# Attention scores shifted by VectorE in every second step, and the gates mixed tile by tile

## The chip, the cores and the metric

The kernel runs on one core of one Trainium2 chip. The metric is the device time of one execution in microseconds. Three runs of the kernel before gave 3368.48, 3369.95 and 3369.95 us; the median is 3369.95 us.

## The reference, cut to what matters

Two layers of graph network and feed-forward block over 3327 nodes with 256 features. The change touches only the last feed-forward block's attention. It has 4 heads (64 wide each) with 4 experts per head: for each head the keys and values are shared, the queries differ by expert, and a causal softmax is taken over 3327 positions. A gate (softmax over the 4 experts) mixes the experts' outputs.

```python
q = einsum('bnsd,neod->bneso', sx, wq); k = einsum('bnsd,nod->bnso', sx, wk); v = einsum('bnsd,nod->bnso', sx, wv)
att = softmax(einsum('bnesd,bntd->bnest', q, k) * d ** 0.5 + causal, axis=-1)
qkv = where(pad[:, :, None], 0.0, einsum('bnest,bntd->bnesd', att, v))
out = transpose(qkv, (0, 1, 3, 2, 4)).reshape(b, nh, s, ne * d)
gs = softmax(einsum('bnsf,nef->bnse', out, gate_w) + gate_b[None, :, None, :], axis=-1)
mixed = einsum('bnsed,bnse->bnsd', out.reshape(b, nh, s, ne, d), gs)
```

The inputs are float32 and so is the softmax. A row's maximum must be known before its exponentials are taken.

## The kernel before, in words

**Units.** `stage_attention` works on two heads at a time (a pair `hp`, 0 or 1). The 3328 positions are cut into query blocks `b`: block 0 has 256 columns, blocks 1 to 6 have 512. A unit `(hp, b, e)` is one query block of one expert `e` for both heads (in block 0 two experts share a unit). There are 52 units. Unit (hp, b, e) has 4b + 2 groups, one for each tile `t` of 128 keys that the block may see, two groups to a step: 1, 3, 5, 7, 9, 11 and 13 steps in blocks 0 to 6. That makes 776 groups. "Units of five steps or more" are those of blocks 2 to 6: 40 units. In a unit the last three groups are narrower (384, 256 and 128 of the 512 columns) because of the causal mask.

**One group.** TensorE makes the scores of 128 keys by 512 queries for both heads (`scores`, L1749: three passes of high and low halves, `klo*qhi`, `khi*qlo`, `khi*qhi`; L1752: a fourth pass that multiplies ones by `nm`, the row of negated maxima, and so subtracts each query's maximum; L1758 adds the causal mask in the diagonal groups). Each pass is two matmuls, one for each head, that run side by side. ScalarE takes the exponential from PSUM into `pt` (L1843, four buffers). TensorE multiplies by the values (`values`, L1770) and GpSimd adds `pt` into the denominators `acc` (`add_up`, L2052; the first group of a unit is a copy, L2049). In the last two units VectorE does that sum instead (L1956).

**Row maxima.** Two units ahead, TensorE makes scores with queries as rows (`row_max`, L1736), and VectorE takes their maxima (L1906, L1910, L1915, L1917). These pieces and the scores share three PSUM slots in a fixed rotation (`slot_users`, `take_slot`): each user waits until the reader of three users ago is done.

**Order of a step** (loops written out by hand, one for each engine): TensorE does [a turn of the next unit's maxima], the first piece of row maxima, the scores of groups g+2 and g+3, the remaining pieces (one or two), the late turns, then the values of groups g and g+1. Turns are small jobs through `psX`: new keys ("k"), new queries ("q"), the row of maxima ("r") and the unit's result ("t"). VectorE does the pieces, then its part of the turns, then a piece of the gates. Each engine's queue is in order.

**Gates.** Once the four experts of a block are done, `gate_pieces` places three pieces on the first unit of the next block, in steps 2, 3 and 4 where it has five steps or more. Piece 0 on VectorE (L1966 to L1979) makes the logits, ScalarE takes their exponential, piece 1 (L1983 to L1986) makes the weights `wgt`, GpSimd multiplies the whole block by them (L2059, 128x2048), and piece 2 on VectorE sums the four experts (L1991), adds them to `hn` (L1997), and takes the statistics for the layer norm (L2001, L2005), all for the whole block.

## Time and profile before

| What | Value |
|---|---|
| Median of three runs | 3369.95 us |
| Profiled execution's own time | 3364.28 us |
| Its span, first to last instruction | 3362.6 us |
| Instructions | 45520 |
| TensorE busy | 2953.1 us (88%) |
| VectorE busy | 1898.3 us (56%) |
| ScalarE busy | 1254.0 us (37%) |
| GpSimd busy | 1772.2 us (53%) |
| TensorE's mean granted clock | 0.934 |

The attention stage runs from about 1095 us (first exponential at 1095.5) to about 3215 us. Busy time is the union of an engine's instructions. Idle time in square brackets or behind a bar is that of the engine just before the instruction, with the instruction whose end released it.

### The profile page before, as it was taken

How to read it: one execution, taken by the hardware profiler on the slowest of the kernel's cores; microseconds unless marked ns; L12 is line 12 of the kernel's file. 1: busy time of each engine (PE TensorE's matmuls, PEld its weight loads, DVE VectorE, ACT ScalarE, POOL GpSimd, SP SyncE). 2: the span in 40 equal slices, each digit the busy share in tenths (PEclk: the TensorE clock that was granted, in tenths of full speed). 3: DMA queues.
4: the chain of work that ended last, by engine and by line, in shares of the span. 5: the costliest groups of instructions: out<-in, count | busy, mean ns of one | idle time of the engine just before them, and what ended most of it. 6: DMA issues, size and time to landing. Idle time of an engine off the chain costs nothing. (4 is left out here: it accounts for less than half of the span.)

```text
span 3362.6 us, 45520 instructions
## 1 busy us (share of the span) xinstructions
PE 2953.1 (88%) x17338; PEld 1822.7 (54%) x17338; DVE 1898.3 (56%) x3632; ACT 1254.0 (37%) x1712; POOL 1772.2 (53%) x956
## 2 busy tenths in 40 slices
PE   7998987679997889899999999788988999999953
PEld 3467666468885455555555555455555554545532
DVE  3555764487733465665655651245656565565566
ACT  2232320355633233343434344323433443434433
POOL 0030020233220357778889899636687888888014
PEclk9999888889998899999999999888999999999976
DMA  9961100299970000000000000000000000000001
GB/s 391 423 246 41 63 1 8 87 290 282 268 130 18 1 1 1 1 1 1 1 1 1 1 4 1 1 1 1 1 1 1 1 1 1 1 1 1 1 8 36
DMA packets 63624, 195.20 MB, mean 58 GB/s; under 512 B 8244, under 2 KB 25010, under 8 KB 53427
## 3 DMA queue, kind: packets, MB, share of 16 engines
q1 hardware_dynamic: 38658, 147.98, 11.4%
q0 software_dynamic: 24752, 44.31, 7.3%
q8 instruction: 143, 2.34, 0.3%
q14 instruction: 71, 0.57, 0.1%
HBM read 188.86 MB, written 3.41 MB: 57 GB/s over the span
## 5 line engine op out<-in xcount | busy, mean ns | idle before, releaser
L2052 POOL TENSOR_TENSOR at_acc<-at_acc,at_pt 128x1024 f32<-128x1024 f32 (+3 forms) x674 | 1445.8, 2145 | 257.4 <-ACT at_pt L1843 178.0
L1843 ACT ACTIVATE at_pt<-at_psR 128x1024 f32<-128x1024 f32 (+3 forms) x776 | 697.8, 942 | 993.2 <-PE at_psR L1752 686.7
L1906 DVE TENSOR_REDUCE at_mx<-at_psR 128x2 f32<-128x1024 f32 x576 | 702.1, 1225 | 493.5 <-PE at_psR L1736 492.0
L1770 PE MATMUL at_psO<-at_pt,v 128*64 128x512 f32 (+3 forms) x3104 | 716.5, 584 | 2.1 <-DVE at_oT L1939 1.8
L1736 PE MATMUL at_psR<-at_khi,at_qhi 64*128 64x512 f32 (+3 forms) x1568 | 353.5, 447 | 134.4 <-DVE at_mx L1906 91.4
L1736 PEld LDWEIGHTS at_psR<-at_khi,at_qhi 64*128 64x128 f32 x1568 | 155.8, 189 | 411.8 <-issue 360.2
L1770 PEld LDWEIGHTS at_psO<-at_pt,v 128*64 128x64 f32 x3104 | 194.2, 140 | 339.6 <-issue 239.1
L1316 PE MATMUL ga_acc<-h,ga_ring 128*128 128x257 f32 (+1 forms) x1352 | 304.7, 385 | 31.0 <-ACT ga_ring L1210 27.3
L1749 PE MATMUL at_psR<-at_qhi,at_klo 64*128 64x512 f32 (+2 forms) x1552 | 307.8, 392 | 6.6 <-ACT at_pt L1843 5.7
L1316 PEld LDWEIGHTS ga_acc<-h,ga_ring 128*128 128x128 f32 (+1 forms) x1352 | 257.3, 192 | 76.6 <-ACT ga_ring L1210 36.0
L1749 PE MATMUL at_psR<-at_qlo,at_khi 64*128 64x512 f32 (+2 forms) x1552 | 294.7, 375 | 0.0
L1749 PE MATMUL at_psR<-at_qhi,at_khi 64*128 64x512 f32 (+2 forms) x1552 | 294.0, 374 | 0.0
L1752 PE MATMUL at_psR<-at_nm,at_ones_r 64*128 64x512 f32 (+2 forms) x1552 | 293.3, 372 | 0.0
L1189 POOL DMA_DIRECT2D ga_ring<-in_adjT x91 | 110.2, 1381 | 252.5 <-DVE ga_ring L1252 247.3
L1910 DVE TENSOR_REDUCE at_mx<-at_psR 128x2 f32<-128x256 f32 (+1 forms) x152 | 102.9, 677 | 185.0 <-PE at_psR L1736 185.0
L345 PE MATMUL gc_acc<-gc_cols,gc_xs 128*128 128x512 f32 x416 | 182.8, 602 | 22.8 <-DVE gc_xs L413 12.6
L1749 PEld LDWEIGHTS at_psR<-at_qhi,at_klo 64*128 64x128 f32 x1552 | 149.2, 188 | 54.0 <-issue 39.2
L1749 PEld LDWEIGHTS at_psR<-at_qhi,at_khi 64*128 64x128 f32 x1552 | 148.6, 187 | 27.2
L1752 PEld LDWEIGHTS at_psR<-at_nm,at_ones_r 64*128 64x128 f32 x1552 | 148.4, 186 | 27.0
L1210 ACT ACTIVATE ga_ring<-ga_ring,f 128x512 f32<-128x512 f32 (+1 forms) x182 | 114.6, 682 | 128.7 <-DMA ga_ring<-in_adjT 128.7
L1749 PEld LDWEIGHTS at_psR<-at_qlo,at_khi 64*128 64x128 f32 x1552 | 148.8, 187 | 24.8
L345 PEld LDWEIGHTS gc_acc<-gc_cols,gc_xs 128*128 128x128 f32 x416 | 80.1, 193 | 124.6 <-issue 112.8
(335 smaller groups left out, 3531.3 us busy)
## 6 DMA issues: line engine op xcount, KB each, us to landing
gc_rows<-in_adj SPq DMA_DIRECT2D x26, 1664.0 KB, 17.4
ga_rows<-in_adj SPq DMA_DIRECT2D x26, 1664.0 KB, 9.9
ga_ring<-in_adjT POOLq DMA_DIRECT2D x78, 512.0 KB, 23.6
gc_cols<-in_adjT SPq DMA_DIRECT2D x26, 1024.0 KB, 14.9
gc_ring<-in_adjT SPq DMA_DIRECT2D x26, 512.0 KB, 8.2
gc_ring<-in_adjT SPq DMA_DIRECT2D x13, 256.0 KB, 2.8
ga_ring<-in_adjT POOLq DMA_DIRECT2D x13, 256.0 KB, 11.0
out_x<-X SPq DMA_DIRECT2D x6, 512.0 KB
```

Of the source, the lines that this page charges most:

```text
L345: ins = pe.matmul(acc[:, b, c, :], xs[:, t, c * P:(c + 1) * P], cols[:, t % COLS, b * BLK:(b + 1) * BLK], start=(t == 0), stop=(t == NT - 1))
L1189: pool.dma_start(ring[:, k, :, 0:w], srcT[:, k, :, c0:c0 + w], accum_op=ALU.add).then_inc(pair_added[k], 16)
L1210: ins = act.activation(ring[:, k, j, 0:w], ring[:, k, j, 0:w], ACT.Exp, bias=f20[:, 2 * k + j:2 * k + j + 1])
L1316: ins = pe.matmul(acc[:, bank(b, s), 0:DM + 1], ring[0:r, k, j, s * P:(s + 1) * P], h1[0:r, 2 * k + j, :], start=(k + j == 0), stop=last)
L1736: ins = pe.matmul(psR[:, slot, l, 0:w], qhi[lanes[l], u % 3, s * P:(s + 1) * P], khi[lanes[l], kc:kc + w], start=True, stop=True)
L1749: pe.matmul(packed(psR[:, slot, l, 0:w], g), left[lanes[l], kc:kc + P], columns(right[lanes[l], u % 3, :], g), start=first, stop=False)
L1752: ins = pe.matmul(packed(psR[:, slot, l, 0:w], g), ones_r[lanes[l], :], columns(nm[lanes[l], u % 2, :], g), start=False, stop=not diag)
L1770: ins = pe.matmul(columns(psO[lanes[l], :], g), v1[:, t, (2 * hp + l) * D:(2 * hp + l + 1) * D], packed(pt[:, g % PTS, l, 0:w], g), start= ...
L1843: act.activation(pt[:, g % PTS, :, 0:w], psR[:, slot_of["score", g] % SLOTS, :, 0:w], ACT.Exp).then_inc(e_ready, 1)
L1906: dve.tensor_reduce(mx[:, u % 2, :, s, c:c + 1].rearrange("p l o -> p (l o)"), got[:, :, 0:w], AX.X, ALU.max).then_inc(p1_read, 1)
L1910: dve.tensor_reduce(mx[:, u % 2, :, s, c:c + 1].rearrange("p l o -> p (l o)"), got[:, :, 0:w - P], AX.X, ALU.max)
L2052: pool.tensor_tensor(to, to, got, ALU.add).then_inc(added, 1)
```

## The change

In units of five steps or more, every second group but the first of these (`t` odd, `t` over 1: 320 of the 776 groups) loses the fourth pass. VectorE instead adds the negated maxima to the scores, from PSUM into `pt` (`take_shifted`), and ScalarE takes the exponential in place in `pt`. For this, each such unit has the row of negated maxima spread to all partitions once: one more pass of ones into a PSUM slot (`spread`) and a ScalarE copy into `shift`.

The gates' last part goes by tiles of 128 positions: GpSimd weighs a tile (`weigh`, steps 3 and 4), VectorE sums a tile's experts ahead of `take_shifted` in steps 5, 6, 7 and 8 counted from the block's first unit (4, 5, 5, 6 in block 2), and its statistics come at the end of that step. The add of the gate's bias disappears: the bias is a fifth column of the sum. Buffers are shared to make room.

```diff
@@ placing
+def block_weighed(u, k):
+        if ls >= 5:
+            return [(hp, b, s) for s in range(SUB) if k == 3 + s // 2]
+        return [(hp, b, s) for s in range(SUB)] if ls == 1 else []
+SUM_STEPS = {5: (4, 5, 5, 6), 7: (5, 6, 7, 8)}
+def block_summed(u, k):
+    if not u or ls < 5 or e > 1:
+        return block_weighed(u, k)
+    hp, b, _ = UNITS[u - 1 - e]
+    return [(hp, b, s) for s in range(SUB) if SUM_STEPS.get(ls, (5, 6, 7, 8))[s] == k + e * ls]
+def shifted_by_vector(g):
+    u, t, _, _ = GROUPS[g]
+    return spread_row(u) and t % 2 == 1 and t > 1
@@ slot_users
+            if k == steps_of(u) - 1 and u + 1 in SPREAD:
+                out.append(("spread", u + 1))
@@ take_slot
+                elif before in SHIFTED_UPTO:
+                    pe.wait_ge(taken, SHIFTED_UPTO[before] + 1)
@@ tensor, scores
-                    for l in range(2):
-                        ins = pe.matmul(... ones_r[lanes[l], :], columns(nm[lanes[l], u % 2, :], g), ...)
+                    if not by_vector:
+                        for l in range(2):
+                            ins = pe.matmul(... ones_r[lanes[l], :], columns(nm[lanes[l], u % 2, :], g), ...)
+                def spread(u):
+                    pe.wait_ge(x_read, turn_of["r", u] + 1)
+                    slot = take_slot(pe, ("spread", u))
+                    for l in range(2):
+                        ins = pe.matmul(psR[:, slot, l, :], ones_r[lanes[l], :], nm[lanes[l], u % 2, :], ...)
+                    ins.then_inc(b_full, 1)
@@ scalar
+                def spread(u):
+                    i = SPREAD.index(u)
+                    act.wait_ge(b_full, i + 1)
+                    if i:
+                        act.wait_ge(taken, sum(1 for g in SHIFTED if g < FIRST[u]))
+                    act.activation(shift[:, :, :], psR[:, slot, :, :], ACT.Copy).then_inc(b_ready, 1)
                 def exps(g):
+                    if g in SHIFTED_UPTO:
+                        act.wait_ge(taken, SHIFTED_UPTO[g] + 1)
+                        act.activation(pt[:, g % PTS, :, 0:w], pt[:, g % PTS, :, 0:w], ACT.Exp).then_inc(e_ready, 1)
+                        return
@@ vector
+                def take_shifted(g):
+                    dve.wait_ge(s_full, g + 1)
+                    dve.wait_ge(b_ready, SPREAD.index(u) + 1)
+                    dve.wait_ge(pv_done, g - PTS + 1)
+                    dve.wait_ge(added, g - PTS + 1)
+                    dve.tensor_tensor(pt[:, g % PTS, :, 0:w], psR[:, slot, :, 0:w],
+                                      shift[:, :, off:off + w], ALU.add).then_inc(taken, 1)
                         link(dve.tensor_reduce(gl ... gp ...))
-                        link(dve.tensor_tensor(gl[:, 0:ws, :], gl[:, 0:ws, :], gb_sb ..., ALU.add))
+                def sum_of_experts(hp, b, s):
+                    dve.wait_ge(weighed, n)
+                    dve.wait_ge(p1_read, pieces[0])
+                    link(dve.tensor_reduce(scrap, on[:, s, :, :].rearrange("p e c -> p c e"), AX.X, ALU.add))
+                    dve.tensor_tensor(there, there, scrap, ALU.add).then_inc(mix_done, 1)
@@ vector, a step
-                        for half in range(2):
-                            for piece in max_pieces(u, k, half):
-                                row_max(u + 2, *piece)
+                        for piece in max_pieces(u, k, 0):
+                            row_max(u + 2, *piece)
+                        if steps_of(u) >= 5:
+                            for x in summed:
+                                sum_of_experts(*x)
+                        if FIRST[u] + 2 * k + 3 in SHIFTED_UPTO:
+                            take_shifted(FIRST[u] + 2 * k + 3)
+                        for piece in max_pieces(u, k, 1):
+                            row_max(u + 2, *piece)
                         for x in late_turns(u, k):
                             turn(*x)
                         for x in gate_pieces(u, k):
                             gate(*x)
+                        for hp, b, s in summed:
+                            link(statistics(hp, QBLOCKS[b][0] // P + s))
@@ gpsimd
-                        pool.tensor_tensor(both, both, wgt ..., ALU.mult)      # 128x2048, a whole block
+                def weigh(hp, b, s):
+                    pool.tensor_tensor(both, both, wgt ..., ALU.mult)          # 128x512, one tile
```

## Rows read from the trace of the kernel before

**Rows 1.** The page, part 1.

```profile
PE 2953.1 (88%) x17338; PEld 1822.7 (54%) x17338; DVE 1898.3 (56%) x3632; ACT 1254.0 (37%) x1712; POOL 1772.2 (53%) x956
```

**Rows 2.** Windows of units: us, busy PE, PEld, DVE, ACT, POOL with counts, PEclk, DMA.

```profile
2615.10:2659.70 44.60, 43.20 (x302) 24.26 (x300) 23.48 (x41) 18.97 (x25) 36.86 (x17) 1.00 0.01 1
2749.90:2812.00 62.10, 54.23 (x358) 29.59 (x356) 39.64 (x73) 22.51 (x29) 50.61 (x23) 0.95 0.00 1
2812.00:2865.00 53.00, 51.60 (x358) 28.89 (x356) 28.21 (x45) 22.72 (x30) 46.08 (x22) 1.00 0.00 1
2972.60:3043.20 70.60, 62.67 (x414) 33.79 (x412) 44.75 (x77) 26.40 (x34) 60.64 (x28) 0.95 0.00 1
3043.20:3103.80 60.60, 59.75 (x414) 33.21 (x412) 32.69 (x48) 26.25 (x33) 55.29 (x26) 1.00 0.00 1
3103.80:3156.80 53.00, 52.89 (x360) 28.17 (x358) 31.82 (x37) 25.76 (x31) 3.71 (x3) 1.00 0.01 1
3156.80:3206.30 49.50, 49.50 (x338) 26.23 (x336) 29.49 (x26) 24.96 (x30) 0.00 (x0) 1.00 0.00 1
3011.50:3014.00 2.50, 2.48 (x6) 0.84 (x8) 1.46 (x5) 0.00 (x0) 2.36 (x2) 0.50 0.00 0
```

**Rows 3.** Groups by line and form on GpSimd in the attention stage.

```profile
L2052 POOL TENSOR_TENSOR at_acc<-at_acc,at_pt 128x1024 f32<-128x1024 f32 x532 | 1264.5, 2377 | 226.8 <-ACT at_pt L1843 166.4 <-POOL at_acc L2052 1.7
```

**Rows 4.** TensorE in order of time, three steps of unit (1, 6, 0).

```profile
2998.94 0.50 PE L1736 MATMUL at_psR<-at_khi,at_qhi 64*128 64x512 f32 x2
2999.74 0.39 PE L1749 MATMUL at_psR<-at_qhi,at_khi 64*128 64x512 f32 x2
2999.97 0.40 PE L1752 MATMUL at_psR<-at_nm,at_ones_r 64*128 64x512 f32 x2
3001.43 1.94 PE L1770 MATMUL at_psO<-at_pt,v 128*64 128x512 f32 x8
3003.30 0.50 PE L1736 MATMUL at_psR<-at_khi,at_qhi 64*128 64x512 f32 x2
3011.52 0.79 PE L1736 MATMUL at_psR<-at_khi,at_qhi 64*128 64x512 f32 x2 [5.86 <-DVE at_mx L1906]
3012.25 3.63 PE L1770 MATMUL at_psO<-at_pt,v 128*64 128x512 f32 x8
3015.81 0.50 PE L1736 MATMUL at_psR<-at_khi,at_qhi 64*128 64x512 f32 x2
```

**Rows 5.** VectorE in order of time, the same unit.

```profile
2993.03 1.89 DVE L1975 TENSOR_TENSOR at_gl<-at_gl,at_gb 128x32 f32<-128x32 f32 x1
3002.93 3.82 DVE L1991 TENSOR_REDUCE at_mixed<-at_on 128x512 f32<-128x2048 f32 x1 [0.16 <-POOL at_on L2059]
3006.78 1.51 DVE L1997 TENSOR_TENSOR hn<-hn,at_mixed 128x512 f32<-128x512 f32 x1
3008.33 1.11 DVE L2001 BATCH_NORM_STATS2 at_hn_stats<-hn 128x6 f32<-128x64 f32 x8
3009.47 0.64 DVE L2005 BATCH_NORM_AGGREGATE hn_mv<-at_hn_stats 128x2 f32<-128x6 f32 x8
```

**Rows 6.** GpSimd in order of time, the same unit.

```profile
2989.99 4.88 POOL L2052 TENSOR_TENSOR at_acc<-at_acc,at_pt 128x1024 f32<-128x1024 f32 x2 [0.91 <-ACT at_pt L1843]
2999.27 3.63 POOL L2059 TENSOR_TENSOR at_on<-at_on,at_wgt 128x2048 f32<-128x2048 f32 x1 [4.40 <-DVE at_wgt L1986]
```

**Rows 7.** Groups by line and form on VectorE in the attention stage.

```profile
L1906 DVE TENSOR_REDUCE at_mx<-at_psR 128x2 f32<-128x1024 f32 x576 | 702.1, 1225 | 493.5 <-PE at_psR L1736 492.0
L1887 DVE TENSOR_TENSOR at_klo<-at_psX,at_khi 128x512 fp32r<-128x512 f32 x11 | 7.6, 692 | 36.5 <-ACT at_khi L1814 36.5
L1968 DVE TENSOR_TENSOR at_gp<-at_onx,at_rden 128x128 f32<-128x128 f32 x12 | 3.5, 292 | 0.4
```

**Rows 8.** ScalarE in order of time at the end of unit (1, 4, 2).

```profile
2704.51 1.95 ACT L1843 ACTIVATE at_pt<-at_psR 128x1024 f32<-128x1024 f32 x2 [3.36 <-PE at_psR L1752]
2707.16 0.60 ACT L1818 ACTIVATE at_qhi<-at_psX 128x512 fp32r<-128x512 f32 x1 [0.70 <-PE at_psX L1701]
```

More of the change, by code:

```diff
@@ L1555, in turn_numbers, with spread_row @@
     return {x: i for i, x in enumerate(every + LAST_TURNS)}
+def shifted_by_vector(g):
+    u, t, _, _ = GROUPS[g]
+    return spread_row(u) and t % 2 == 1 and t > 1
+def spread_row(u):
+    return steps_of(u) >= 5
+SHIFTED = [g for g in range(FIRST[NU]) if shifted_by_vector(g)]
+SHIFTED_UPTO = {g: i for i, g in enumerate(SHIFTED)}
+SPREAD = [u for u in range(NU) if spread_row(u)]
 def slot_users():
@@ L1641, in block_number, with tiles_upto @@
             return hp * NQB + b
+        def tiles_upto(hp, b):
+            return sum(w // P for i in range(hp + 1) for _, w in QBLOCKS[:b if i == hp else NQB])
         def columns(ap, g):
@@ L1672, in take_slot @@
                 what, before = users[i - SLOTS]
-                pe.wait_ge(p1_read if what == "max" else e_ready, before + 1)
+                if what == "max":
+                    pe.wait_ge(p1_read, before + 1)
+                elif what == "spread":
+                    pe.wait_ge(b_ready, SPREAD.index(before) + 1)
+                elif before in SHIFTED_UPTO:
+                    pe.wait_ge(taken, SHIFTED_UPTO[before] + 1)
+                else:
+                    pe.wait_ge(e_ready, before + 1)
             return i % SLOTS
@@ L1746, in scores @@
                     diag = t * P >= QBLOCKS[b][0]
-                    for left, right, first in ((klo, qhi, True), (khi, qlo, False), (khi, qhi, False)):
+                    by_vector = g in SHIFTED_UPTO
+                    for left, right, n in ((klo, qhi, 0), (khi, qlo, 1), (khi, qhi, 2)):
                         for l in range(2):
-                            pe.matmul(packed(psR[:, slot, l, 0:w], g), left[lanes[l], kc:kc + P],
-                                      columns(right[lanes[l], u % 3, :], g), start=first, stop=False)
-                    for l in range(2):
-                        ins = pe.matmul(packed(psR[:, slot, l, 0:w], g), ones_r[lanes[l], :],
-                                        columns(nm[lanes[l], u % 2, :], g), start=False, stop=not diag)
+                            ins = pe.matmul(packed(psR[:, slot, l, 0:w], g), left[lanes[l], kc:kc + P],
+                                            columns(right[lanes[l], u % 3, :], g), start=n == 0,
+                                            stop=n == 2 and by_vector and not diag)
+                    if not by_vector:
+                        for l in range(2):
+                            ins = pe.matmul(packed(psR[:, slot, l, 0:w], g), ones_r[lanes[l], :],
+                                            columns(nm[lanes[l], u % 2, :], g), start=False, stop=not diag)
                     if diag:
@@ L1799, in _ @@
                             row_max(u + 2, *piece)
+                        if k == steps_of(u) - 1 and u + 1 in SPREAD:
+                            spread(u + 1)
                         for x in late_turns(u, k):
@@ L1863, in _ @@
                             exps(g + 3)
+                        if k == steps_of(u) - 1 and u + 1 in SPREAD:
+                            spread(u + 1)
                         for x in late_turns(u, k):
@@ new lines, in gate, with statistics @@
+                        dve.tensor_tensor(wgt[:, 0:ws, :, :], gl[:, 0:ws, :].rearrange("p s (l g) -> p s g l", l=2),
+                                          rden[:, 0:ws, 0:NE, :], ALU.mult).then_inc(gate_ready, 1)
+                def statistics(hp, tile):
+                    for l in range(2):
+                        ins = dve.bn_stats(hn_stats[:, l, :], hn[:, tile, hp * P + l * D:hp * P + (l + 1) * D])
+                    link(ins)
+                    for l in range(2):
+                        ins = dve.bn_aggr(hn_mv[:, tile, 2 * hp + l, :], hn_stats[:, l, :])
+                    return ins
@@ new lines, in last_sum @@
+                def last_sum():
+                    hp, b = NPR - 1, NQB - 1
+                    t0, n = QBLOCKS[b][0] // P, tiles_upto(NPR, 0)
+                    dve.wait_ge(weighed, n)
+                    link(dve.tensor_tensor(on[:, :, 0:2, :], on[:, :, 0:2, :], on[:, :, 2:4, :], ALU.add))
+                    link(dve.tensor_tensor(on[:, :, 0, :], on[:, :, 0, :], on[:, :, 1, :], ALU.add))
+                    there = hn[:, t0:t0 + SUB, hp * P:(hp + 1) * P]
+                    dve.tensor_tensor(there, there, on[:, :, 0, :], ALU.add).then_inc(mix_done, SUB)
+                    dve.wait_ge(mix_done, n)
+                    for s in range(SUB):
+                        link(statistics(hp, t0 + s))
@@ L2082, in _ @@
                             add_up(FIRST[u] + 2 * k + 1)
-                        for x in gate_pieces(u, k):
-                            gate(*x)
+                        for x in block_weighed(u, k):
+                            weigh(*x)
 class FfnWeights:
```

110 lines of the change are left out of this document (58 added, 52 removed).

## The prediction

> **What bounds the kernel now.** I read the page's busy times first. TensorE is busy 2953.1 us of 3362.6 and no other engine passes 56% [rows 1]. The change touches only the attention stage, so next I cut that stage into units with the windows view, since a unit's length depends on its block. Three kinds of unit stand out [rows 2].
> (a) Ordinary units. (1, 4, 1) takes 44.6 us with TensorE busy 43.20, and (1, 5, 1) takes 53.0 with 51.60, both at clock 1.00. TensorE sets their length.
> (b) Block 6. (1, 6, 1) takes 60.6 us, TensorE is busy 59.75 and GpSimd 55.29. Two GpSimd adds back to back take 4.88 us [rows 6] at a mean of 2.377 each [rows 3], so there is about 0.13 us between them. With 26 such gaps GpSimd needs 58.7 us. Its backlog from the unit before takes most of the rest, so GpSimd sets the pace of this unit. The same holds for the other block-6 units in which GpSimd adds up, six in both pairs.
> (c) First units of a block, where the previous block's gates fall. (1, 5, 0) takes 62.1 against 53.0 of its neighbour, (1, 6, 0) 70.6 against 60.6, with TensorE idle about 8 us in each.
>
> In order of time (c) becomes plain [rows 4, 5]. A plain step, from one first row-maximum piece to the next, is 2998.94 to 3003.30, 4.36 us. The step after it runs from 3003.30 to 3015.81, 12.51 us: VectorE sits 7.2 us in the last gate piece (3.82 + 1.51 + 1.11 + 0.64 and gaps), the PSUM slot isn't freed and TensorE idles 5.86 us. Then the clock stands at 0.50 of full, that is at 1.2 GHz [rows 2], and the values that took 1.94 us take 3.63. One block's last gate piece so costs 12.51 - 4.36 = 8.15 us.
>
> **The passes that go.** Two passes start at 2999.74 and 2999.97 [rows 4]: passes are pipelined, so a full one costs its pitch of 0.23 us and not its duration of 0.40. A unit of n steps loses n - 1 passes, the last two of them of 384 and 128 columns, together one full pass: n - 2 full ones. Over 8 units each of 5, 7, 9, 11 and 13 steps that is 8 x (3 + 5 + 7 + 9 + 11) = 280 passes, 64.4 us. The spread adds one pass to each of 40 units, some 0.25 us with its weights: -10. The ScalarE copy of 128x1024 takes about 1 us (two exponentials take 1.95 [rows 8]). ScalarE ends its exponentials at 2706.46 and idles 0.70 us before the copy of the new queries at 2707.16. The spread's copy fills that and moves it by some 0.35, 0.25 of which is the pass already counted: -4 in 40 units. Left: 50.4 us.
>
> **What of it doesn't reach the end.** In the six GpSimd-bound units, 11 full passes at 0.23 less the spread, about 2.3 us each, go: -13.7. Block 5's ordinary units have GpSimd at 46.08 + 22 x 0.13 = 48.9 of 53.0. In plain steps its pitch of two adds, 5.0 us, is longer than TensorE's 4.36, and four `pt` buffers cover only so much. I give back 0.5 in six units: -3. In unit (1, 6, 3) VectorE does the denominators. It will have two adds and one shifted add a step, 3 x 1.225 = 3.7 us against 49.5 / 13 = 3.8 us now, so that unit gains 1 and not 2.3: -1.3. In steps that VectorE bounds (next part), 26 outside block 6 have a pass to lose: -6. Units with three pieces in a step: -2. So 24.4 us are worth something.
>
> **The shifted add.** It is a tensor_tensor of 128x1024 with one input in PSUM and one in SBUF. The nearest rows are the same form at 512 elements, 692 ns, and a 1024-element read of PSUM, 1225 ns [rows 7]. I take 1.225; the bounds are that and that plus a whole GpSimd add (2.38), if the two engines got in each other's way. In a plain step VectorE has two pieces, 2.45 us; with the shifted add 3.7, below TensorE's 4.13. It is hidden there. The add sits between the first and the second piece in VectorE's queue, so behind it wait the later pieces, the queries' low half and the gates. The second piece's slot is next wanted one step on, by the second score group, 3.4 us after the shifted group's end, and VectorE frees it after 2.6. ScalarE's exponential then comes 1.3 us later and reads SBUF; it is busy 22.72 of 53.0, and the values that need it are a step away. Bounds for that exponential: as now, or up to 0.3 us more; neither shows.
>
> **The gates.** Removed: 8.15 us of stall and slow clock in each block. Block 6 is apart, so eight blocks: +65. Added, for a tile on VectorE: the sum 3.82 / 4 = 0.96; the add into `hn`, two SBUF inputs of 128 elements, 0.29 by [rows 7] plus a wait for GpSimd; statistics (1.11 + 0.64) / 4 = 0.44; links 0.1. That wait is the unknown. The bias add of 32 elements took 1.89 us at 2993.03 and ended at 2994.92, just after GpSimd's add at 2994.87 [rows 5, 6], a wait of 1.7. The add into `hn` of 512 elements took 1.51, against 0.69 for that size: 0.82. It can be between 0 and 2.38. I take 0.82, the row of the same instruction. A tile is then 2.6 us, and its step is 2.45 + 1.225 + 2.6 = 6.3 us for VectorE against 4.36 now: VectorE bounds it, +1.95. Four such steps cost 7.8 in block 5. In the smaller blocks some fall on a last step without a shifted add or on a step that a turn already lengthens; I take 7, 6 and 6 for blocks 4, 3 and 2. Both pairs: -54. TensorE then idles under 2.2 us at a time. At 5.86 us the clock fell afterwards, and I count on no fall here. Gate pieces 0 and 1 come behind one shifted add each, some 0.5 a block: -4. The bias add is gone, but the subtraction that ends piece 0 also has two SBUF inputs and is then the one that meets GpSimd's add: gain nothing. Sum of the gates: +7.
>
> The Trainium skill, SBUF — State Buffer, section "SBUF: two separate sides", says that VectorE and GpSimd take their shared port pair by an exclusive lock for a whole instruction, and that among 1x VectorE instructions only those with two SBUF inputs take it. The row at 2993.03 agrees (1.89 us, ending with the GpSimd add), and by that rule the shifted add (PSUM and SBUF) is free of it, as the 692 ns row has it, while four adds into `hn` in place of one take it four times.
>
> **Block 6's first units.** GpSimd waits 4.40 us for the weights and weighs in 3.63 [rows 6], and from there its adds set the time. The weights come about 1 us later and four tile multiplies have three more gaps: -3 in both pairs. Single-step and three-step units, the joint with the second pair and the tail: 0, within 3 us either way.
>
> **Sum.** 24.4 + 7 - 3 = 28 us. The profiled execution took 3364.28 us, so 3336; the median of the runs is 5.7 above it: 3342 us.
>
> **Rivals.**
> 1. The tile steps cost more than the lump did. Mechanism: each add into `hn` meets a GpSimd add early, and waits 1.7 us as at 2993.03. That is 0.88 more in 40 steps, 35 us: 3377. A whole add each time gives 1.56 x 40 = 62: 3404. It turns slower than before from 0.7 us more a tile on, a wait of 1.5. For it: the kernel repeats the same phases, and most bias adds waited so long. Against: the `hn` rows waited half that. Chance 0.20.
> 2. The tiles fit in VectorE's gaps. It idles 1.9 us in a plain step now. If the wait is nil in most and TensorE runs ahead in the slots, a tile step costs 1.1 and not 1.95: 26 us better, 3316. Chance 0.15.
> 3. GpSimd's pace spreads. With plain steps at 4.13 us and GpSimd at 5.0, blocks 4 and 5 run out of `pt` buffers, 12 units lose their pass gain of 1.5 each, and the slots cost 5 more: 3365. Chance 0.12.
> 4. The shifted adds wait for GpSimd, against the 692 ns row: 1.2 us more on average, VectorE 4.9 in a plain step, 0.5 to 0.8 over today's in some 200 steps: over 3450. Chance 0.03.
> The forecast has 0.50. That the passes aren't gone is excluded by the code.
>
> **Numbers.** A change under 0.2%, 6.7 us, can't be told from none; that is 3363 to 3377. Faster: 0.48 + 0.15 + 0.04 = 0.67. Same: 0.02 + 0.08 + 0.02 = 0.12. Slower: 0.18 + 0.03 = 0.21. The range for 8 in 10 reaches from rival 2's 3316, a little below, to past rival 1's first price: 3312 to 3386. The forecast's own is 3330 to 3358.
>
> **What would show it.** L1752's matmuls fall by 640 and 80 appear for the spread. Steps without gates in blocks 2 to 5 last 4.13 us; the (b, 1) units of blocks 4 and 5 get shorter by about 1.5 us; block 6's don't. The 5.86 us idle of TensorE is gone, with the clock at 1.00 there. In its place stand four steps of about 6.3 us in which TensorE waits for VectorE. Shifted adds are 1.22 us each. I am wrong if a plain step isn't shorter, if the `hn` adds wait over 1.5 us, if the clock falls in the tile steps, or if first units of a block stay as long as they are in every block.

## The result, and the profile after

Six runs of the kernel after gave 3383.4 to 3418.3 us, median 3391.9. Beside them six runs of the kernel before gave 3363.1 to 3370.0, median 3368.4. The ratio of the means is 1.0087, with a 95% interval of 1.0046 to 1.0128. By the medians the change made the kernel 23 us slower (29 us by the means), where 28 us faster was forecast. The profiled execution took 3411.98 us with a span of 3410.3. On a second chip the same kernel took 3408.0 against 3363.7. The kernel after scatters over 35 us and the one before over 7. In its six runs the granted clock goes with the time, from 0.928 (3418 us) to 0.940 (3383 us).

The page of the kernel after, part 1:

```profile
PE 2966.7 (87%) x16778; PEld 1797.0 (53%) x16778; DVE 2271.8 (67%) x4008; ACT 1323.7 (39%) x1754; POOL 1775.5 (52%) x992
```

Against [rows 1], TensorE has 560 matmuls less (640 gone, 80 new) and yet is busy no less. Part of that is time at the lower clock, below. VectorE has 373 us more.

Windows of the kernel after, with the columns of [rows 2]: units (1, 4, 1), (1, 5, 0), (1, 5, 1), (1, 6, 0), (1, 6, 1), (1, 6, 2) and (1, 6, 3).

```profile
2646.90:2694.00 47.10, 44.28 (x288) 23.61 (x286) 33.78 (x55) 20.61 (x27) 37.13 (x19) 0.96 0.00 1
2785.00:2852.00 67.00, 55.87 (x340) 28.99 (x340) 55.48 (x88) 24.54 (x30) 52.04 (x27) 0.95 0.00 1
2852.00:2906.40 54.40, 52.27 (x340) 27.96 (x338) 38.04 (x54) 24.60 (x30) 44.12 (x20) 0.97 0.00 1
3014.80:3088.50 73.70, 62.06 (x394) 32.10 (x393) 62.78 (x94) 28.73 (x35) 62.41 (x32) 1.00 0.00 1
3088.50:3149.30 60.80, 59.29 (x395) 32.09 (x392) 44.91 (x60) 28.37 (x33) 54.18 (x24) 1.00 0.00 1
3149.30:3200.90 51.60, 50.48 (x336) 26.11 (x334) 42.29 (x46) 28.00 (x32) 3.83 (x3) 1.00 0.00 1
3200.90:3250.10 49.20, 48.83 (x326) 24.81 (x322) 42.14 (x39) 27.40 (x31) 0.00 (x0) 1.00 0.00 1
```

First units of a block got longer, (1, 5, 0) from 62.1 to 67.0 and (1, 6, 0) from 70.6 to 73.7. VectorE is busy 55.48 and 62.78 there, where it was busy 39.64 and 44.75. The second units, which were to get shorter by 1.5, got longer too: (1, 4, 1) from 44.6 to 47.1 and (1, 5, 1) from 53.0 to 54.4. Of the units shown, the expected gain of TensorE shows only in (1, 6, 2).

**Tile steps.** VectorE in order of time in unit (1, 5, 0) of the kernel after, one step with a tile:

```profile
2825.75 1.23 DVE L1998 TENSOR_REDUCE at_mx<-at_psR 128x2 f32<-128x1024 f32 x1
2827.08 1.06 DVE L2100 TENSOR_REDUCE at_gp<-at_on 128x128 f32<-128x512 f32 x1
2828.17 1.99 DVE L2102 TENSOR_TENSOR hn<-hn,at_gp 128x128 f32<-128x128 f32 x1
2830.20 1.22 DVE L2045 TENSOR_TENSOR at_pt<-at_psR,at_shift 128x1024 f32<-128x1024 f32 x1
2831.34 1.22 DVE L1998 TENSOR_REDUCE at_mx<-at_psR 128x2 f32<-128x1024 f32 x1
2832.47 0.34 DVE L2090 BATCH_NORM_STATS2 at_hn_stats<-hn 128x6 f32<-128x64 f32 x2
2832.85 0.25 DVE L2093 BATCH_NORM_AGGREGATE hn_mv<-at_hn_stats 128x2 f32<-128x6 f32 x2
2833.13 1.23 DVE L1998 TENSOR_REDUCE at_mx<-at_psR 128x2 f32<-128x1024 f32 x1
```

The step runs from 2825.75 to 2833.13, 7.38 us without a pause of VectorE; 6.3 were forecast. It is one of the long ones: the eight tile steps of (0, 5, 0) and (1, 5, 0) last 5.4 to 7.4 us and 6.3 on average, and the eight of block 6's first units 6.3 to 7.5 and 7.0 on average. TensorE in the same stretch waits twice, first for the maxima and then for the shifted add:

```profile
2827.12 0.50 PE L1790 MATMUL at_psR<-at_khi,at_qhi 64*128 64x512 f32 x2 [0.84 <-DVE at_mx L1998]
...
2831.57 0.50 PE L1804 MATMUL at_psR<-at_qhi,at_klo 64*128 64x512 f32 x2 [1.67 <-DVE at_pt L2045]
```

The second wait is new in kind. The slot of a shifted group is freed by VectorE, behind the tile's work, and no longer by ScalarE. The shifted adds and the adds into `hn` by source line (duration ns min/median/max):

```profile
L2045 DVE TENSOR_TENSOR at_pt<-at_psR,at_shift x320: 412/1224/1226, 1228.9 to 3249.2; 128x1024 f32<-128x1024 f32 x120, 128x768 f32<-128x768 f32 x40
...
  POOL at_acc L2173: 50.3, 19
```

```profile
L2102 DVE TENSOR_TENSOR hn<-hn,at_gp x48: 291/1194/2386, 1161.1 to 3070.5; 128x128 f32<-128x128 f32 x48
```

A full shifted add takes 1.22 us every time. The add into `hn` takes 0.29 at best, 2.39 at worst, 1.19 in the median. The kernel run again (the run called again, below) has at the place of 2828.17 this row:

```profile
2827.59 0.52 DVE L2102 TENSOR_TENSOR hn<-hn,at_gp 128x128 f32<-128x128 f32 x1
```

The length of a step from the first matmul of one step's values to that of the next, in the first unit (1, 5, 0):

| step | 1 | 2 | 3 | 4 | 5 | 6 | 7 | 8 | 9 | 10 |
|---|---|---|---|---|---|---|---|---|---|---|
| before | 6.39 | 5.75 | 5.75 | 4.40 | 10.78 | 6.44 | 4.20 | 4.53 | 4.20 | 5.09 |
| gates_only (below) | 6.39 | 5.75 | 5.38 | 4.39 | 4.36 | 5.13 | 5.74 | 5.12 | 5.13 | 5.07 |
| after | 6.24 | 5.61 | 6.77 | 5.50 | 4.21 | 6.59 | 7.21 | 7.12 | 5.41 | 7.38 |
| again (below) | 6.24 | 5.60 | 6.77 | 5.48 | 4.21 | 5.69 | 5.73 | 7.60 | 4.95 | 5.78 |

The lump is gone from steps 5 and 6. The tiles lengthen steps 6 to 9. Beside them steps 3 and 4, behind the first gate pieces, and step 10 got longer too.

**The new keys' step.** In a block's second unit TensorE also projects the keys of the next block. In the unit (1, 5, 1), kernel before:

```profile
2830.78 0.70 PE L1691 MATMUL at_psX<-sxT,at_wk 128*128 128x256 f32 x2 [0.55 <-ACT at_onx L1832]
2831.41 1.94 PE L1770 MATMUL at_psO<-at_pt,v 128*64 128x512 f32 x8
```

The same place in the kernel after:

```profile
2871.62 0.97 PE L1745 MATMUL at_psX<-sxT,at_wk 128*128 128x256 f32 x2 [1.00 <-ACT at_onx L1900]
2872.51 3.31 PE L1834 MATMUL at_psO<-at_pt,v 128*64 128x512 f32 x8
```

ScalarE's copy `at_onx`, which frees `psX`, now stands behind an exponential that waited for a shifted add. TensorE waits 1.00 us and not 0.55, the granted clock falls to 0.50 (2872.5 to 2874.0), and the values take 3.31 us. This step and the next last 7.58 and 5.59 us where they lasted 7.00 and 4.36. Both units (0, 5, 1) and (1, 5, 1) show that fall in after and in again.

**Steps with three pieces.** In the ordinary unit (1, 4, 2) a pass that goes can leave no gain at all. All engines in order of time, kernel before:

```profile
2672.12 1.94 PE L1770 MATMUL at_psO<-at_pt,v 128*64 128x512 f32 x8
...
2674.97 0.39 PE L1752 MATMUL at_psR<-at_nm,at_ones_r 64*128 64x512 f32 x2
...
2675.40 1.94 ACT L1843 ACTIVATE at_pt<-at_psR 128x1024 f32<-128x1024 f32 x2 [2.71 <-PE at_psR L1752]
...
2676.10 0.97 PE L1736 MATMUL at_psR<-at_khi,at_qhi 64*128 64x512 f32 x4
...
2678.45 1.94 PE L1770 MATMUL at_psO<-at_pt,v 128*64 128x512 f32 x8
```

The same step in the kernel after:

```profile
2706.90 1.94 PE L1834 MATMUL at_psO<-at_pt,v 128*64 128x512 f32 x8
...
2709.73 0.41 PE L1809 MATMUL at_psR<-at_nm,at_ones_r 64*128 64x512 f32 x2
...
2710.18 1.03 ACT L1922 ACTIVATE at_pt<-at_psR 128x1024 f32<-128x1024 f32 x1 [2.23 <-PE at_psR L1809]
...
2710.63 0.49 PE L1790 MATMUL at_psR<-at_khi,at_qhi 64*128 64x512 f32 x2
...
2711.35 0.50 PE L1790 MATMUL at_psR<-at_khi,at_qhi 64*128 64x512 f32 x2 [0.23 <-ACT at_pt L1922]
...
2713.23 1.94 PE L1834 MATMUL at_psO<-at_pt,v 128*64 128x512 f32 x8
```

Both take 6.33 us from values to values. The third piece of a step goes into the slot of the step's first score group. That slot is free when the group's exponential ends, at 2711.21. In the kernel before, the last two pieces ran back to back: the second group's four passes brought TensorE there just when the first exponential of the two (1.94 us together, from 2675.40) was done. Now they are three, TensorE arrives earlier and waits 0.23 us, the very pitch of the pass. The nine steps of this unit, in the version with the spread alone (below) and in the kernel after:

| step | 1 | 2 | 3 | 4 | 5 | 6 | 7 | 8 | 9 |
|---|---|---|---|---|---|---|---|---|---|
| spread alone | 4.03 | 6.41 | 6.32 | 4.40 | 4.93 | 4.36 | 5.08 | 4.20 | 6.69 |
| after | 4.02 | 6.24 | 6.33 | 4.21 | 4.93 | 4.29 | 5.07 | 4.21 | 6.69 |

The sum of the differences is 0.43 us. Seven full passes at 0.23 were counted, 1.61. Steps 3, 5, 7 and 9 have three pieces and gain nothing; steps 3, 5 and 7 hold 2.75 of the seven passes. The plain steps 2 and 4 gain 0.17 and 0.19. Step 1, which begins with a wait for the new queries, gains nothing either; why wasn't looked into. The unit (1, 6, 2) has no pieces at all, and there the whole pitch arrives: its plain steps fall from 3.92 us to 3.69.

Where the time went, from one profiled execution of each kernel but the last three: the difference to the kernel before in us, by class of unit, cut at the first exponential of each unit ("tile units" are the 14 first and second units whose steps hold the gates of blocks 1 to 5). The last column is for the tile units alone: the time that the granted clock stood at its lower level, 1.2 GHz, there.

| kernel | before the stage | blocks 0, 1 | tile units | other units of blocks 2 to 5 (20) | other units of block 6 | behind the last exponential | sum | lower clock, tile units |
|---|---|---|---|---|---|---|---|---|
| before | | | | | | | | 78.5 |
| after | +6.4 | +6.4 | +14.6 | +15.2 | +1.1 | +4.0 | +47.7 | 71.7 |
| again | +5.9 | +6.5 | +6.6 | +18.8 | +2.5 | +3.3 | +43.5 | 75.1 |
| gates_only | -3.2 | +5.1 | -39.0 | +4.5 | +3.0 | -0.7 | -30.4 | 23.9 |
| spread_only | +3.7 | +3.5 | -32.3 | +22.0 | +5.9 | +3.3 | +6.2 | 23.9 |
| shift_only | +3.0 | -5.1 | +20.2 | +10.7 | -0.6 | +5.0 | +33.2 | 92.2 |
| spread_after_q | +1.5 | +2.4 | +4.3 | -1.0 | -2.5 | +3.3 | +7.8 | 68.3 |
| shift_only_late | +0.2 | -4.0 | +6.6 | -4.4 | -1.3 | +3.5 | +0.5 | 99.0 |
| late_no_hn_add | +3.8 | -7.0 | -30.3 | 0.0 | -0.5 | +3.3 | -30.8 | 44.4 |
| partial | +6.2 | +3.6 | -35.4 | +0.4 | -0.5 | +1.9 | -24.0 | 41.0 |
| late_not_in_tile_units | -2.1 | +7.2 | -39.2 | +3.0 | +0.1 | +4.4 | -26.7 | 23.9 |

The column before the stage holds no change at all; so a difference of 6 us in one column of one execution is scatter. The rest of the reading goes by terms that are larger, or by medians, or by units that repeat in all executions.

One such sum repeats. The 16 third and fourth units of blocks 2 to 5 lose 96 full passes, 22 us at the pitch. With shifted adds they are 4.9 and 4.8 us shorter than without (after and again against spread_only) and 4.8 and 5.0 us in two more pairs (spread_after_q and late_not_in_tile_units against gates_only, late spread included). So a good fifth of what was counted arrives there.

The last column shows a part of the loss that no single wait shows. Gates by tiles alone take the time at the lower clock in the tile units from 78.5 us to 23.9; with shifted adds it is back at 71.7. At the lower clock the values take 3.63 us and not 1.94 [rows 4], so a microsecond there costs TensorE half a microsecond at most. An estimate from this: of the 46.9 us that lie between spread_only and after in the tile units, up to 24 can be clock. What clock and waits cost apart from each other no run shows.

### The profile page after: what moved, and what is told of

It reads as the page before. It is cut to its first block and busy times, and to the rows that moved or that the text cites. A ratio compares the mean times of both kernels' runs of the same rounds, so it can differ in the third digit from the quotient of the medians.

```text
span 3410.3 us, 45343 instructions
## 1 busy us (share of the span) xinstructions
PE 2966.7 (87%) x16778; PEld 1797.0 (53%) x16778; DVE 2271.8 (67%) x4008; ACT 1323.7 (39%) x1754; POOL 1775.5 (52%) x992
## 5 line engine op out<-in xcount | busy, mean ns | idle before, releaser
L1922 ACT ACTIVATE at_pt<-at_psR 128x1024 f32<-128x1024 f32 (+1 forms) x456 | 433.4, 961 | 659.1 <-PE at_psR L1809 470.4
L1790 PE MATMUL at_psR<-at_khi,at_qhi 64*128 64x512 f32 (+3 forms) x1568 | 367.1, 462 | 116.9 <-DVE at_mx L1998 65.0
L1916 ACT ACTIVATE at_pt<-at_pt 128x1024 f32<-128x1024 f32 (+1 forms) x320 | 304.4, 951 | 417.6 <-DVE at_pt L2045 417.6
L2045 DVE TENSOR_TENSOR at_pt<-at_psR,at_shift 128x1024 f32<-128x1024 f32 (+1 forms) x320 | 348.8, 1090 | 163.7 <-PE at_psR L1804 87.8
L1804 PE MATMUL at_psR<-at_qhi,at_klo 64*128 64x512 f32 (+2 forms) x1552 | 315.4, 401 | 33.1 <-DVE at_pt L2045 29.3
L1316 PE MATMUL ga_acc<-h,ga_ring 128*128 128x257 f32 (+1 forms) x1352 | 304.7, 385 | 30.4 <-ACT ga_ring L1210 27.0
L1809 PE MATMUL at_psR<-at_nm,at_ones_r 64*128 64x512 f32 (+3 forms) x912 | 176.6, 380 | 0.0
```

The source lines that it names most:

```text
L1316: ins = pe.matmul(acc[:, bank(b, s), 0:DM + 1], ring[0:r, k, j, s * P:(s + 1) * P], h1[0:r, 2 * k + j, :], start=(k + j == 0), stop=last)
L1790: ins = pe.matmul(psR[:, slot, l, 0:w], qhi[lanes[l], u % 3, s * P:(s + 1) * P], khi[lanes[l], kc:kc + w], start=True, stop=True)
L1804: ins = pe.matmul(packed(psR[:, slot, l, 0:w], g), left[lanes[l], kc:kc + P], columns(right[lanes[l], u % 3, :], g), start=n == 0, stop=n ...
L1809: ins = pe.matmul(packed(psR[:, slot, l, 0:w], g), ones_r[lanes[l], :], columns(nm[lanes[l], u % 2, :], g), start=False, stop=not diag)
L1916: act.activation(pt[:, g % PTS, :, 0:w], pt[:, g % PTS, :, 0:w], ACT.Exp).then_inc(e_ready, 1)
L1922: act.activation(pt[:, g % PTS, :, 0:w], psR[:, slot_of["score", g] % SLOTS, :, 0:w], ACT.Exp).then_inc(e_ready, 1)
```

## The experiments

They ran in three groups of four in the order below, each group on one chip beside the kernel before, whose medians were 3363.7, 3363.7 and 3365.1 us. Differences are of medians; across groups those of the ratios stand up to 2 us from them. The edits are to the kernel after unless said.

**again**: the kernel after unchanged, for a base on the same chip.

> The changed kernel once more. Its six times ran from 3383 to 3418 us with a mean granted clock of 0.928 to 0.940, while the kernel before stays within 7 us. Theory S (where the spread stands costs the time) says nothing of that scatter. Theory C (the tile steps leave TensorE waiting and its clock falls in some of them, in some executions) expects this profile to have its clock dips at other places than the first profile, and the units whose clock is 1.00 in both to have the same length in both within 0.2 us. Time expected: 3383 to 3418 us, median about 3392.

Measured: 3408.0 us (3400.9 to 3409.9), ratio 1.0123 (1.011 to 1.0136).

**gates_only**: the gates by tiles, no spread and no shifted adds.

```diff
 def spread_row(u):
-    return steps_of(u) >= 5
+    return False
```

> Only the gates go tile by tile; all scores keep their fourth pass and nothing is spread. Theory S: the loss comes from the spread and the shifted adds, so this is faster than before by the lump's 8.15 us per block less tile steps of 2.45 + 2.6 = 5.1 us for VectorE against 4.36: 8 blocks x (8.15 - 4 x 0.7) = -43, about 3325 us. Theory G (the tiles are the loss): 3380 or more.

Measured: 3336.1 us (3333.9 to 3339.3), ratio 0.9914 (0.9901 to 0.9927). The gates alone gain 28 us. The 43 us that were expected didn't come: tile steps last 5.1 to 5.7 us, and what lies outside the tile units got some 9 us longer. Everything that is lost against the kernel before comes with VectorE's adds and what they need.

**shift_only**: the kernel before with the spread and the shifted adds (and buffers shared to make room).

```diff
+SPREAD = [u for u in range(NU) if spread_row(u)]
@@ vector, a step (kernel before)
+                        if FIRST[u] + 2 * k + 3 in SHIFTED_UPTO:
+                            take_shifted(FIRST[u] + 2 * k + 3)
```

> Only the shifted adds and the spread; the gates stay whole blocks (their sum goes into the buffer of the turned-out unit, to make room in SBUF). By the prediction's terms: 3369 - 24 = 3345 us. Theory S: last steps of a unit are longer by 0.7 (two pieces) to 1.0 us (three) and plain steps shorter by 0.17, so ordinary units are 0.5 us longer, not shorter: 3369 + 10 to 20 = 3379 to 3389 us. Theory G: 3350 us or less.

Measured: 3396.9 us (3395.9 to 3397.8), ratio 1.0094 (1.0081 to 1.0107). The half of the change that takes 640 matmuls from TensorE costs 33 us without the new gates, more than the 10 to 20 expected.

**spread_after_q**: the spread behind the late turns on TensorE and on ScalarE.

```diff
-                        if k == steps_of(u) - 1 and u + 1 in SPREAD:
-                            spread(u + 1)
                         for x in late_turns(u, k):
                             turn(*x)
+                        if k == steps_of(u) - 1 and u + 1 in SPREAD:
+                            spread(u + 1)
```

> The changed kernel with the spread's pass and its ScalarE copy behind the late turns instead of ahead of them. Theory S: the chain new queries (TensorE), high half (ScalarE), low half (VectorE), next row maxima (TensorE) is no longer put off by the spread, so the last step of a unit goes back from 5.8 to about 5.3 us (two pieces) and from 6.7 to 5.9 (three): 40 units x 0.5 to 0.8 = 20 to 30 us off, 3365 us. Theory G: within 5 us of the changed kernel.

Measured: 3378.0 us (3371.0 to 3385.8), ratio 1.0042 (1.0028 to 1.0057): 30 us less than again. The order in two queues is worth as much as the whole gain that was forecast. End of unit (1, 4, 2), all engines, kernel after:

```profile
2741.14 0.49 PE L1824 MATMUL at_psR<-at_nm,at_ones_r 64*128 64x512 f32 x2 [0.54 <-ACT at_pt L1922]
...
2741.57 1.12 PE L1755 MATMUL at_psX<-sxT,at_wq 128*128 128x512 f32 x2
2741.68 1.02 ACT L1910 ACTIVATE at_shift<-at_psR 128x1024 f32<-128x1024 f32 x1 [0.68 <-PE at_psR L1824]
...
2742.73 0.60 ACT L1884 ACTIVATE at_qhi<-at_psX 128x512 fp32r<-128x512 f32 x1
...
2744.11 0.50 PE L1790 MATMUL at_psR<-at_khi,at_qhi 64*128 64x512 f32 x2 [0.61 <-DVE at_qlo L1983]
```

The same place with the spread behind the queries:

```profile
2707.57 1.13 PE L1755 MATMUL at_psX<-sxT,at_wq 128*128 128x512 f32 x2
...
2708.62 0.51 PE L1824 MATMUL at_psR<-at_nm,at_ones_r 64*128 64x512 f32 x2
...
2708.73 0.60 ACT L1884 ACTIVATE at_qhi<-at_psX 128x512 fp32r<-128x512 f32 x1 [0.71 <-PE at_psX L1755]
...
2709.22 1.02 ACT L1910 ACTIVATE at_shift<-at_psR 128x1024 f32<-128x1024 f32 x1
...
2710.10 0.50 PE L1790 MATMUL at_psR<-at_khi,at_qhi 64*128 64x512 f32 x2 [0.18 <-DVE at_qlo L1983]
```

From the start of the queries' pass (L1755) to the next unit's row maxima are 2.54 us with the spread in front and 2.53 behind it; the saving lies ahead. In front, the spread first waits 0.54 us for its slot, and the queries' pass waits behind it. Behind, that wait and the spread's pass fall into the time in which TensorE waits for the queries anyway. The last step of (1, 4, 2) is 6.69 us with the spread in front and 6.10 behind it, and the first of the next unit 4.03 and 3.61: 1.01 us together.

**spread_only**: gates and spread, no shifted adds.

```diff
 def shifted_by_vector(g):
-    return spread_row(u) and t % 2 == 1 and t > 1
+    return False
```

With it goes ScalarE's wait for shifted adds ahead of the copy.

> The changed kernel with its spreads (pass, ScalarE copy, old place ahead of the late turns) but without a shifted add: every score group keeps its fourth pass, nobody reads the spread row. Beside the kernel with gates only (3336 us) it prices 40 spreads. Theory S: 0.7 to 1.0 us each, 28 to 40 us: 3364 to 3376 us, last steps of a unit at 5.8 and 6.7 us. The prediction's price (0.35 us each, 14 us): 3350 us.

Measured: 3369.0 us (3357.7 to 3375.7), ratio 1.0014 (1.0004 to 1.0025). Against gates_only that is 33 us for 40 spreads, 0.8 each. The last step of (1, 4, 2) grows from 5.66 to 6.69 by the spread alone.

**shift_only_late**: shift_only with the spread behind the late turns (the edit of spread_after_q).

> Whole-block gates, shifted adds, and the spread behind the late turns. Beside the same with the spread ahead (3397 us). Theory S: 30 us less, 3367 us, about the kernel before, since 0.17 us a plain step is what the shifted adds win and the gate lump grows by the shifted add's 1.2 us (10.8 to 12.4 us step). A rival (the spread's place matters only beside tile gates, where VectorE is full): 3385 us or more.

Measured: 3369.4 us (3364.1 to 3378.0), ratio 1.0016 (1.0006 to 1.0026), 28 us less than shift_only. The place of the spread is worth about the same with either form of the gates.

**late_no_hn_add**: spread_after_q without each tile's add into `hn`, so its result leaves out the attention's part of almost every tile. It is there for its time alone.

```diff
-                    link(dve.tensor_reduce(scrap, ..., AX.X, ALU.add))
-                    there = hn[:, tile, hp * P:(hp + 1) * P]
-                    dve.tensor_tensor(there, there, scrap, ALU.add).then_inc(mix_done, 1)
+                    dve.tensor_reduce(scrap, ..., AX.X, ALU.add).then_inc(mix_done, 1)
```

> The kernel with the spread behind the late turns (3378 us), less the 48 adds of a tile into hn, so the residual sum is left out. Theory L (these adds, 1.27 us each on average with the wait for GpSimd, lie on the path in the tile steps because VectorE bounds them): 40 x 1.3 = 50 us less would be the most, with steps of 6.8 falling to 5.5: 3330 us. Rival (TensorE or GpSimd takes over at once): 3360 us or more.

Measured: 3334.3 us (3333.6 to 3342.2), ratio 0.9918 (0.9906 to 0.9931). The 48 adds of 128 elements cost 44 us, 0.9 each, in steps that VectorE bounds. Of it 34.6 lie in the tile units by the table (+4.3 to -30.3), where the time at the lower clock fell too, from 68.3 us to 44.4. What these adds cost without shifted adds beside them wasn't run, so the 44 us aren't all of the collision.

**partial**: the spread late, shifted adds only in third and fourth units of blocks 3 to 5 and in (1, 6, 2).

```diff
-    return steps_of(u) >= 5
+    return steps_of(u) >= 7 and UNITS[u][2] >= 2 and (UNITS[u][1] < NQB - 1 or u == NU - 2)
```

> Gates tile by tile everywhere, but the shifted adds only where neither gate tiles nor GpSimd's pace stand in the way: the third and fourth expert's units of blocks 3 to 5, and (1, 6, 2); 13 units, spread behind the late turns. These units were 0.3 to 0.6 us shorter than before in that kernel, (1, 6, 2) 1.4. Theory S with L: 12 x 0.45 + 1.4 = 7 us less than gates only (3336): 3329 us. Rival (a spread in an ordinary unit costs what the adds win): 3334 to 3338 us, no difference.

Measured: 3335.0 us (3330.2 to 3340.3), ratio 0.9911 (0.9896 to 0.9925). The gain of some 7 us that was hoped for over gates_only doesn't show in the time. In the profiled execution it is there: the 13 units with shifted adds are 7.4 us shorter than in gates_only together, (1, 6, 2) alone 1.6. The same execution is 9.4 us longer ahead of the stage, where nothing changed, and 3.6 us longer in the tile units. With intervals of 0.15% on either side, 5 us, the two medians can't decide it.

**late_not_in_tile_units**: the spread late, shifted adds everywhere but in tile units.

```diff
-    return steps_of(u) >= 5
+    return steps_of(u) >= 5 and UNITS[u][2] >= (1 if steps_of(u) >= 9 else 2)
```

> The kernel with late spreads (3378 us), but no spread and no shifted add in the units that hold gate pieces or tiles (first units of all blocks, second units of blocks 2 and 3); the tiles stay. Theory V (VectorE has too little room for tile and shifted add in one step): all that the shifted adds cost sits in those 12 units: 3335 us, as with gates only. Rival (the cost is spread over all 40 units): 12 of 40 units free of it, 3378 - 0.3 x 42 = 3365 us.

Measured: 3338.3 us (3337.1 to 3343.8), ratio 0.9922 (0.9909 to 0.9936), 40 us less than spread_after_q and not less than gates_only. The expectation speaks of 12 units without shifted adds; the edit makes it 14. So shifted adds beside tiles cost 40 us, and all others together, even with a spread that costs next to nothing, gain nothing that shows in the time. Unit (1, 5, 0) in gates_only, in late_no_hn_add and here, windows with the columns of [rows 2]:

```profile
2725.70:2783.50 57.80, 53.66 (x366) 29.98 (x362) 43.77 (x78) 22.87 (x29) 47.99 (x24) 1.00 0.00 1
```

```profile
2728.50:2787.80 59.30, 51.87 (x338) 27.61 (x336) 48.27 (x83) 24.43 (x30) 49.39 (x26) 1.00 0.00 1
```

```profile
2725.60:2783.50 57.90, 53.76 (x366) 30.12 (x362) 43.44 (x78) 22.92 (x30) 48.28 (x25) 1.00 0.00 1
```

The clock is 1.00 in all three and was 0.95 in the kernel before, in the one after and in again.

The last three runs ask whether the tile form of the gates can be bettered.

**gates_one_add**: gates_only, with the tiles' sums kept and one add and all statistics with the last tile.

```diff
+                    if s == ws - 1:
+                        there = hn[:, tile - s:tile + 1, hp * P:(hp + 1) * P]
+                        link(dve.tensor_tensor(there, there, mixed[:, 0:ws, :], ALU.add))
```

> Gates only (3336 us), the tiles summed into a buffer of their own, one add into hn and all statistics of a block at its last tile. Theory L (each add's wait for GpSimd counts): three waits of 0.8 us and three adds less in each of 10 blocks, but a lump of about 1.5 + 2.4 us at the last tile: 3336 - 10 = 3326 us at best. Rival (the lump gives it back): 3333 to 3340 us.

**gates_spaced**: gates_only with tile steps further apart in blocks 4 to 6.

```diff
-SUM_STEPS = {5: (4, 5, 5, 6), 7: (5, 6, 7, 8)}
+SUM_STEPS = {5: (4, 5, 5, 6), 7: (5, 6, 7, 8), 9: (4, 5, 6, 7), 11: (4, 6, 8, 9), 13: (5, 7, 9, 11)}
```

> Gates only (3336 us) with the tile sums of blocks 5 and 6 in every second step (4, 6, 8, 9 and 5, 7, 9, 11) and those of block 4 one step earlier, off the unit's last step. Theory V: a plain step has 1.9 us of VectorE to spare and a tile needs 2.9, so every second step leaves no excess; block 5's tile steps cost 0.7 to 1.3 us each now, and block 4's last one put off the next unit's first step by 2.3: 2 x (3 + 3) + some in block 6, which GpSimd paces: 3324 us. Rival (GpSimd's pace, 5.0 us a step, takes over): 3333 us or more.

**gates_spaced_one_add**: both edits.

> Both together. If the two gains are of different microseconds: 3336 - 10 - 12 = 3314 us. If both take the same excess away: 3324 us.

Measured: 3341.5 us (3339.4 to 3346.1), ratio 0.993 (0.9918 to 0.9943); 3335.3 (3334.5 to 3338.1), 0.9911 (0.9898 to 0.9925); 3344.4 (3339.8 to 3344.7), 0.9934 (0.992 to 0.9948). All three missed what was hoped for; the spaced tiles are within their rival. One add in place of four makes a lump again and costs 5 us; (1, 5, 0) goes from 57.8 to 61.8. Tiles further apart leave that unit at 57.8. Why each tile costs the same wherever it stands wasn't looked into.

The best versions are gates_only, gates_spaced and partial, equal within their scatter and about 28 us faster than the kernel before.

## Why the prediction was wrong, step by step

The median was forecast at 3342 us and came at 3391.9, above the range's 3386. On the chip of the first group the pieces add up: gates alone -28, the spread +33, shifted adds +39, together +44, which is again. The forecast had -38 for the passes, +14 for the spread and -4 for the gates beside shifted adds. So the spread's term was 19 us too small and the rest 53 us off, of which about 20 lie in the 20 other units of blocks 2 to 5 and most of the remainder in the tile units.

- **The passes that go, and with them "Units with three pieces in a step: -2": failed by about 20 us.** After all that it took off, the forecast kept 38.4 us of the 64.4 (64.4 - 13.7 - 3 - 1.3 - 6 - 2), before the spread. The pitch of 0.23 was right, but it was credited to each step. In a plain step 0.16 arrives (4.36 before; in unit (1, 6, 0) of the kernel after first pieces start at 3047.08 and 3051.28, 4.20). In a step with three pieces nothing does: the rotation of three slots ties the third piece to an exponential that was only just hidden. That explains half of what is missing in (1, 4, 2). The 20 other units of blocks 2 to 5 lose 128 full passes, 29 us at their pitch, of which the forecast kept some 24. Against spread_only they got 6.8 us shorter in the kernel after by the table, and 3.2 in again. About 20 us of the forecast are missing here. A part lies in the second units of blocks 4 and 5, where the new keys' step got 1.8 us longer, with a fall of the clock; the forecast had no term for it. In block 6's other units, where the forecast took most of the gain off, its size was right (+5.9 to +1.1, 4.8 us).
- **The spread, "-10" and "-4": failed by 19 us.** Sized at 0.35 us each, it cost 0.8: 33 us and not 14. The copy does fill ScalarE's idle time as forecast, but the spread's pass first waits 0.54 us for a slot, with the queries' pass behind it, and that wait wasn't in the sum. Moved behind the queries the spread costs next to nothing: 1.01 us come back at the end of (1, 4, 2), where it had added 1.03 to the last step.
- **The tile steps, "VectorE bounds it, +1.95": right in mechanism, and nearly in size.** The add into `hn` waited 1.0 us on average against the 0.82 taken, and the sum took 1.06 against 0.96. In (0, 5, 0) and (1, 5, 0) the steps came at 6.3 on average, as forecast, in block 6's first units at 7.0. Rival 1 wanted a wait of 1.5 or more and didn't come. VectorE does free the slot of the shifted scores last, and TensorE stands 1.67 us in the step shown.
- **What shifted adds and tiles cost each other: the step that failed most.** Shifted adds alone beside the old gates cost about what the spread costs (shift_only +33). Together with tiles they cost some 40 us more, taken away by removing the shifted adds in tile units (-40), and by removing the adds into `hn` (-44, with what these cost by themselves). Besides the tile steps three things show in (1, 5, 0). Step 3, behind gate piece 0, lasts 6.77 us and not 5.38, where the forecast had some 0.5 a block: the product in piece 0 waits for GpSimd (see the bias add below). The clock falls at step 4. And step 10, with the spread, lasts 5.78 or 7.38 and not 5.07.
- **"Removed: 8.15 us" in each block: right.** The idle time of 5.86 us is gone, and gates_only shows what it was worth. Its 28 us were forecast as +7 with the shifted adds in the same steps.
- **"I count on no fall here": wrong, a term put at nothing.** In the tile units the time at the lower clock is 71.7 us in the kernel after and 23.9 in gates_only, worth up to 24 us by the estimate above. (1, 6, 0) kept 1.00 in the kernel after with as much waiting, and had 0.98 in again. The clock isn't the whole of the scatter, though. (1, 5, 0) took 67.0 us in the kernel after and 63.0 in again, with a mean clock of 0.95 in both. Of the 4 us, 2.4 are two adds into `hn` that met GpSimd in another phase: 1.20 and 1.99 us against 0.29 and 0.52. The other 1.6 are step 10: the clock was at 0.50 in it in the kernel after (2848.0 to 2851.4), and in again it was at 0.50 in a step that VectorE bounds (2838.1 to 2841.5), where it cost nothing that shows.
- **Block 6's first units, "-3": too small.** They were to get 1.5 us longer each and got 3.0 longer (70.6 to 73.6 in both pairs), with tile steps of 7.0 us. In gates_only they are 2.6 shorter than before (68.0).
- **The six GpSimd-paced units: right.** (1, 6, 1) went from 60.6 to 60.8 with 2.5 us less for TensorE to do.
- **The bias add, "gain nothing": right for this kernel, for another reason.** The wait for GpSimd moved to the product in L2070, two inputs in SBUF:

```profile
2805.96 2.35 DVE L2070 TENSOR_TENSOR at_gp<-at_onx,at_rden 128x160 f32<-128x160 f32 x1
```

On average the product takes 1.80 us in the kernel after and 0.33 in gates_only:

```profile
L2070 DVE TENSOR_TENSOR at_gp<-at_onx,at_rden 128x160 f32<-128x160 f32 x11 | 19.8, 1798 | 0.4
```

```profile
L2070 DVE TENSOR_TENSOR at_gp<-at_onx,at_rden 128x160 f32<-128x160 f32 x12 | 3.9, 325 | 0.4
```

So it isn't the missing bias add that moves the wait. In shift_only, which keeps the bias add, the product takes 1.68 too and the bias add 0.40, where the kernel before has 0.29 and 1.49. The shifted add puts the product into GpSimd's way.

- **Shifted adds at 1.225 us: right**, and rival 4 is excluded: 412 to 1226 ns by size, never longer. The Trainium skill (SBUF — State Buffer, "SBUF: two separate sides") says that outside VectorE's 2-port modes only an instruction with two SBUF inputs takes the port pair shared with GpSimd; the shifted adds, with one input in PSUM, agree: 1.226 us at most, beside GpSimd adds of 2.38. What they did wait for is GpSimd's work, not its port: 50.3 us in 19 waits for `added`, until a `pt` buffer is free, as in the row under L2045. Of it 48.7 us lie in block 6, so rival 3 (blocks 4 and 5 run out of `pt` buffers) didn't come either.
- **Small units, joint and tail, "0, within 3 us": wrong.** The tail got 4.0 us longer, and 3.3 to 5.0 in the other kernels with a spread in every unit. Blocks 0 and 1 got 6.4 and 6.5 longer in the kernel after and in again, 5.1 of it in gates_only too. VectorE carries denominators and shifted adds in (1, 6, 3), and four adds are left behind the last shifted one:

```profile
3249.56 3.60 DVE L2057 TENSOR_TENSOR at_acc<-at_acc,at_pt 128x1024 f32<-128x1024 f32 x4
```

What stays open: why the clock falls in (1, 6, 0) in one execution and not in the next, and how the loss in the tile units divides between waits and clock. The late spread wasn't run without shifted adds; that it costs next to nothing is read from steps and from the pairs with and without the move.

## What to carry to other kernels

An operation taken from the busiest engine is worth its pitch only where nothing else was tied to the same moment. Before counting it n times, take one step of each kind, go through the slot waits behind the removed work, and ask what they have left: here a slot that used to come free just in time swallowed 0.23 us in every such step. A term put at nothing, as the clock was here, needs a row too. An instruction inserted into an in-order queue is priced by the first wait that it adds and by who stands behind it; ask for the other place before the other method. Two changes that load the same queue in the same steps aren't added up: try them apart, since here one gains 28 us, the other loses 33 and the pair loses 44, some 40 more than their sum.
